# Gate multiplications of the experts move from VectorE to GpSimd, in a fused attention and mixture-of-experts kernel

## The reference

```python
# layer 0: group norm, softmax attention over all 4096 tokens of an image, residual
h = group_norm(x, norm_w, norm_b)              # 32 groups
q, k, v = h @ Wq + bq, h @ Wk + bk, h @ Wv + bv
x = x + (softmax(q @ k.T * C ** -0.5) @ v) @ Wo + bo
# layer 1, on tokens t (b, 4096, 128)
# a: causal attention with one fixed query a head, 8 heads
kv = silu(ln(t) @ W_kv.T);  k, v = kv[..., 0], kv[..., 1]
s = einsum('hd,bthd->bth', q_proj, k)
e = exp(s - cummax(s, axis=1))
t = t + (cumsum(e[..., None] * v) / cumsum(e)[..., None]).mean(heads)
# b: 8 experts, the best two of each token
p = softmax(ln(t) @ router_w + router_b)
top_p, top_i = top_k(p, 2);  top_p /= sum(top_p)
t = t + sum_k top_p[k] * (ln(t) @ expert_w[top_i[k]] + expert_b[top_i[k]])
```

## Time and profile before

| what | value |
|---|---|
| median of 3 runs | 2849.72 us |
| the profiled execution | 2849.48 us, span 2847.4 us |
| mean granted TensorE clock | 0.976 |
| TensorE busy | 2651.4 us, 93% |
| VectorE busy | 2260.2 us, 79% |
| ScalarE busy | 1842.4 us, 65% |
| GpSimd busy | 1766.7 us, 62% |
| moved by DMA | 130.76 MB |

### The profile page before, as it was taken

The page is one execution under the profiler, slowest core; times in us unless marked ns, Lnnn a source line. Parts: engine busy times, 40 slices in busy tenths (PEclk is TensorE's granted clock), DMA queues, the critical chain, the costliest instruction groups (busy, mean ns, idle before and its releaser), DMA issues. The chain is left out here.

```text
span 2847.4 us, 37342 instructions
## 1 busy us (share of the span) xinstructions
PE 2651.4 (93%) x11107; PEld 1909.6 (67%) x11107; DVE 2260.2 (79%) x3453; ACT 1842.4 (65%) x3368; POOL 1766.7 (62%) x1457
## 2 busy tenths in 40 slices
PE   6999999999999999999999999778799899899788
PEld 2888877788877788887788888534355455455443
DVE  5788887788887788887788888427888898898996
ACT  4667676666777666677666666657766666665540
POOL 3677777777776777776777777715544444444430
PEclk8999999999999999999999999989999999999989
DMA  1000000100000100000000000034233323223220
GB/s 63 5 12 8 12 12 8 38 12 12 9 12 8 37 13 10 14 8 8 8 16 8 9 16 8 24 93 164 112 116 109 114 103 135 103 73 131 92 75 26
DMA packets 48378, 130.76 MB, mean 46 GB/s; under 512 B 11472, under 2 KB 14096, under 8 KB 38960
## 3 DMA queue, kind: packets, MB, share of 16 engines
q1 hardware_dynamic: 48176, 128.39, 13.1%
HBM read 110.94 MB, written 17.43 MB: 45 GB/s over the span
## 5 line engine op out<-in xcount | busy, mean ns | idle before, releaser
L184 POOL TENSOR_TENSOR p_lo<-pf,p_hi 128x512 fp32r<-128x512 f32 x1024 | 1319.2, 1291 | 426.3 <-ACT p_hi L409 421.1
L404 ACT ACTIVATE pf<-s_ps 128x512 f32<-128x512 f32 x1024 | 612.8, 598 | 528.6 <-PE s_ps L295 527.7
L499 DVE TENSOR_REDUCE mx<-m_ps 128x1 f32<-128x512 f32 x1024 | 702.7, 688 | 301.8 <-PE m_ps L278 297.6
L515 DVE TENSOR_TENSOR sum_ps<-sum_ps,pf 128x512 f32<-128x512 f32 x960 | 661.9, 690 | 22.7 <-ACT pf L404 22.4
L409 ACT CAST p_hi<-pf 128x512 fp32r<-128x512 f32 x1024 | 627.3, 613 | 0.0
L886 POOL TENSOR_TENSOR acc<-acc,ay 128x512 f32<-128x512 f32 x192 | 255.8, 1332 | 280.8 <-DVE ay L1223 280.4
L293 PE MATMUL s_ps<-q_hi,kd_hi 128*128 128x512 f32 x1024 | 425.4, 415 | 0.0
L278 PE MATMUL m_ps<-kp,q_hi 128*128 128x512 f32 x1024 | 405.4, 398 | 11.1 <-DVE mx L499 5.1
L307 PE MATMUL om_ps<-p_hi,v_hi 128*128 128x512 f32 x1024 | 401.1, 392 | 4.6 <-POOL p_lo L184 4.6
L294 PE MATMUL s_ps<-q_hi,kd_lo 128*128 128x512 f32 x1024 | 399.8, 390 | 0.0
L295 PE MATMUL s_ps<-q_lo,kd_hi 128*128 128x512 f32 x1024 | 399.8, 390 | 0.0
(11 more groups left out here) (206 smaller groups left out, 3605.9 us busy)
## 6 DMA issues: line engine op xcount, KB each, us to landing
bq<-weight_rows SPq DMA_DIRECT2D x64, 1024.0 KB, 4.9
xb<-in_x_dram SPq DMA_DIRECT2D x8, 1024.0 KB, 6.1
rb_sb<-inverse_rows SPq DMA_DIRECT2D x32, 256.0 KB, 3.7
tokens<-xb SPq DMA_DIRECT2D x32, 256.0 KB, 2.0
tp<-tokens SPq DMA_DIRECT2D x32, 256.0 KB, 4.9
rb<-norm_rows SPq DMA_DIRECT2D x32, 256.0 KB, 4.2
tv<-tokens SPq DMA_DIRECT2D x32, 256.0 KB, 5.4
out_dram<-tv SPq DMA_DIRECT2D x32, 256.0 KB, 2.4
```

Of the source, the lines that this page charges most:

```text
L184: nc.gpsimd.tensor_tensor(p_lo[:, r, :], pf[:, r, :], p_hi[:, r, :].bitcast(F32), ALU.subtract).then_inc(lo_done, 1)
L404: nc.scalar.activation(pf[:, g % RING, :], s_ps[:, g % 2, :], ACT.Exp, scale=SCALE).then_inc(exp_done, 1)
L499: nc.vector.tensor_reduce(mx[:, n % 2, sub, chunk:chunk + 1], m_ps[:, j % 2, :], AX.X, ALU.max).then_inc(m_max, 1)
L515: nc.vector.tensor_tensor(sum_ps[:], sum_ps[:], p, ALU.add).then_inc(sum_done, 1)
```

## The change

The gate rows no longer come from TensorE. `hold_gates` also copies the turned gates to `l_sb`, SyncE writes 8 rows of each image to DRAM (`gate_rows`) and brings each block's 8 gates back to all 128 partitions, in two halves of four experts and 1 MB each (`gate_spread`, buffer `gb`, called gate_b in the program). GpSimd multiplies them with the tokens (`gated`), so `spread`, `sel` and `g_ps` go. The two banks of `g_ps` become value banks: `v_ps` has four. On GpSimd the addition of head h - 1 stands in slot h, the last one in slot 0 of the next step. On TensorE expert e stands in slot e + 2 (`X_LAG`), the last two in the next step, and `output` in slot 2. The gates are computed one slot earlier or two, and turned in slot 5. The gate matrix is laid out so that the rows for DRAM are the first eight of a group.

```diff
-    V_LAG, F_LAG = 5, 11
+    V_LAG, F_LAG, X_LAG = 5, 11, 2
...
+        gb = sb("gate_b", [C, 2, HALF, TOK])
...
-        gt = sb("gt", [C, 2, TOK], F32R)
+        gt = sb("gt", [C, TOK], F32R)
...
-        v_ps = psum("v_ps", [C, 2, BANK])
+        v_ps = psum("v_ps", [C, 4, BANK])
...
-        g_ps = psum("g_ps", [C, 2, BANK])
...
+            def gate_rows(s):
+                sp.wait_ge(gr_act, s + 1)
+                for b in range(B):
+                    sp.dma_start(gates_d[s, b, :, :], l_sb[QUAD * b:QUAD * b + E, :]).then_inc(gr_out, 16)
+
+            def gate_spread(i, j):
+                s, b, cols = place(i)
+                sp.wait_ge(gr_out, 16 * B * (s + 1))
+                if i:
+                    sp.wait_ge(xg_pool, (i - 1) * E + HALF * (j + 1))
+                sp.dma_start(gb[:, j, :, :].rearrange("p e n -> p (e n)"),
+                             gates_d[s, b:b + 1, HALF * j:HALF * (j + 1), :].rearrange("o e n -> o (e n)")
+                             .to_broadcast([C, HALF * TOK])).then_inc(gb_in[j], 16)
...
-                if stage(f - 1):
-                    store(f - 1)
...
                 if stage(v + 1):
                     weight_spread(v + 1, 1)
+                if stage(f - 1):
+                    store(f - 1)
+                if stage(f + 1):
+                    if (f + 1) % B == 0:
+                        gate_rows((f + 1) // B)
+                    gate_spread(f + 1, 0)
+                    gate_spread(f + 1, 1)
...
+            def gated(f, e):
+                pool.wait_ge(gb_in[e // HALF], 16 * (f + 1))
+                after(pool, x_pe, f * E + e - 2)
+                if e == 0:
+                    pool.wait_ge(t2_dve, f + 1)
+                nc.gpsimd.tensor_tensor(xg[:, (f * E + e) % 3, :], gb[:, e // HALF, e % HALF, :], tv[:, f % NV, :],
+                                        ALU.mult).then_inc(xg_pool, 1)
...
                 for h in range(HEADS):
+                    if h == 0 and stage(v - 1):
+                        add_head(v - 1, HEADS - 1)
+                    if stage(f):
+                        gated(f, h)
                     if stage(k + 1) and h == 1:
                         scaled(k + 1)
                     if stage(k + 1) and h == 5:
                         low(k + 1)
-                    if stage(v):
-                        add_head(v, h)
+                    if stage(v) and h:
+                        add_head(v, h - 1)
...
-                after(pe, y_dve, v * HEADS + h - 1)
-                project(v_ps[:, h % 2, :], h, 1, v).then_inc(v_pe, 1)
+                after(pe, y_dve, v * HEADS + h - 3)
+                project(v_ps[:, h % 4, :], h, 1, v).then_inc(v_pe, 1)
...
-                    if stage(f) and h == 0:
-                        spread(f, 0)
...
-                    if stage(f) and h + 1 < E:
-                        spread(f, h + 1)
...
-                    if stage(f):
-                        if h == 0:
+                    if stage(f - 1) and h < X_LAG:
+                        expert(f - 1, E + h - X_LAG)
+                    if stage(f) and h >= X_LAG:
+                        if h == X_LAG:
                             expert_bias(f)
-                        expert(f, h)
-                    if norm2_at(j, 2) is not None and h == 7:
+                        expert(f, h - X_LAG)
+                    if norm2_at(j, 2) is not None and h == 5:
                         turn_gates(norm2_at(j, 2))
...
                 act.wait_ge(gt_pe, s + 1)
-                nc.scalar.copy(gt[:, s % 2, :], st_ps[:]).then_inc(gt_act, 1)
+                act.wait_ge(lt_pe, s + 1)
+                nc.scalar.copy(l_sb[:], st_ps[:]).then_inc(gr_act, 1)
+                after(act, x_pe, (B * s - 1) * E + 1)
+                nc.scalar.copy(gt[:], st_ps[:]).then_inc(gt_act, 1)
...
-            def gated(f, e):
-                dve.wait_ge(g_pe, f * E + e + 1)
-                after(dve, x_pe, f * E + e - 2)
-                nc.vector.tensor_tensor(xg[:, e % 3, :], g_ps[:, e % 2, :], tv[:, f % NV, :], ALU.mult).then_inc(xg_dve, 1)
...
-                if stage(f - 1):
-                    output(f - 1)
                 for h in range(HEADS):
+                    if stage(f - 1) and h == X_LAG:
+                        output(f - 1)
                     if stage(v):
                         weigh(v, h)
-                    if stage(f):
-                        if h == 0:
-                            gated(f, 0)
-                        if h + 1 < E:
-                            gated(f, h + 1)
```

More of the change, by code:

```diff
@@ L640, in scan_attention_and_experts @@
     rows_d = nc.dram_tensor("weight_rows", (SUPERS, B * 2, HALF, TOK), F32, kind="Internal").ap()
+    gates_d = nc.dram_tensor("gate_rows", (SUPERS, B, E, TOK), F32, kind="Internal").ap()
     rs_d = nc.dram_tensor("norm_rows", (SUPERS, B, TOK), F32, kind="Internal").ap()
@@ L720, in scan_attention_and_experts @@
             sem(n) for n in ("var2_dve", "msq2_act", "ln2_act", "rst2_act", "gate", "th_act"))
-        gt_pe, gt_act, g_pe, xg_dve, x_pe, out_dve = (
-            sem(n) for n in ("gt_pe", "gt_act", "g_pe", "xg_dve", "x_pe", "out_dve"))
+        gt_pe, gt_act, gr_act, gr_out, xg_pool, x_pe, out_dve = (
+            sem(n) for n in ("gt_pe", "gt_act", "gr_act", "gr_out", "xg_pool", "x_pe", "out_dve"))
+        gb_in = [sem(f"gb_in{i}") for i in range(2)]
+        clr = sem("clr")
         block = ctx.enter_context(nc.Block())
@@ L863, in _ @@
             nc.gpsimd.memset(eb_lo[:].bitcast(F32), 0.0).then_inc(cst2, 1)
+            nc.gpsimd.memset(g32[:], 0.0).then_inc(clr, 1)
             def scaled(i):
@@ L973, in row_sums @@
                     mm.then_inc(s_pe, 1)
[L975 to L981, removed]
             def expert_bias(f):
@@ L985, in expert_bias @@
                 after(pe, out_dve, f)
-                pe.matmul(mo_ps[:], eb_hi[:, b, :], gt[:, s % 2, :], start=True, stop=False)
-                pe.matmul(mo_ps[:], eb_lo[:, b, :], gt[:, s % 2, :], start=False, stop=False)
+                pe.wait_ge(gt_act, s + 1)
+                pe.matmul(mo_ps[:], eb_hi[:, b, :], gt[:], start=True, stop=False)
+                pe.matmul(mo_ps[:], eb_lo[:, b, :], gt[:], start=False, stop=False)
             def expert(f, e):
-                pe.wait_ge(xg_dve, f * E + e + 1)
-                pe.matmul(mo_ps[:], ew[:, e, :], xg[:, e % 3, :], start=False, stop=(e == E - 1)).then_inc(x_pe, 1)
+                pe.wait_ge(xg_pool, f * E + e + 1)
+                pe.matmul(mo_ps[:], ew[:, e, :], xg[:, (f * E + e) % 3, :], start=False, stop=(e == E - 1)).then_inc(x_pe, 1)
             pe.wait_ge(cst1, 5)
@@ L1011, in _ @@
             pe.wait_ge(ec_act, 3)
-            pe.wait_ge(cst3, 6)
-            for j in range(STEPS):
+            pe.wait_ge(cst3, 5)
+            for j in range(STEPS + 1):
                 k, v, f = j, j - V_LAG, j - F_LAG
                 for h in range(HEADS):
-                    if stage(f) and h == 0:
-                        spread(f, 0)
                     if stage(v):
                         value(v, h)
-                    if stage(f) and h + 1 < E:
-                        spread(f, h + 1)
                     if stage(k - 1) and h == 0:
@@ L1075, in silu_value @@
                 act.wait_ge(v_pe, v * HEADS + h + 1)
-                nc.scalar.activation(v_ps[:, h % 2, :], v_ps[:, h % 2, :], ACT.Silu).then_inc(v_act, 1)
+                nc.scalar.activation(v_ps[:, h % 4, :], v_ps[:, h % 4, :], ACT.Silu).then_inc(v_act, 1)
             def old_weight(v, h):
@@ L1091, in hold_logits @@
                 act.wait_ge(lg_pe, s + 1)
+                after(act, gr_out, 16 * B * s)
                 nc.scalar.copy(l_sb[:], st_ps[:]).then_inc(lg_act, 1)
@@ L1166, in _ @@
                         high(k + 1)
-                    if norm2_at(j, 2) is not None and h == 4:
+                    if norm2_at(j, 2) is not None and h == 2:
                         s = norm2_at(j, 2)
@@ L1213, in weigh @@
                 dve.wait_ge(v_act, v * HEADS + h + 1)
-                zv = v_ps[:, h % 2, :]
+                zv = v_ps[:, h % 4, :]
                 nc.vector.tensor_tensor(zv, bq[:, q % 3, h % HALF, :], zv, ALU.mult).then_inc(z_dve, 1)
@@ L1278, in gates @@
                                             ALU.add).then_inc(gate, 1)
-                if slot == 1:
+                if slot == 0:
                     ready(3)
                     first_of(lg, top1, place1, pick1, 3)
-                if slot == 2:
+                if slot == 1:
                     ready(8)
@@ L1287, in gates @@
                     first_of(lg, top2, place2, pick2, 9)
-                if slot == 3:
+                if slot == 2:
                     nc.vector.tensor_tensor(gap[:], top1[:], top2[:], ALU.subtract).then_inc(gate, 1)
@@ L1291, in gates @@
                     nc.vector.tensor_tensor(work, pick1[:], pick2[:], ALU.subtract).then_inc(gate, 1)
-                if slot == 5:
+                if slot == 3:
```

(13 more changed lines are left out.)

14 lines of the change are left out of this document (5 added, 9 removed).

## The result

The changed kernel takes 2835.05 us, median of 6 runs (2833.76 to 2839.51), against 2850.45 for the kernel before: a ratio of 0.9946, 95% interval 0.9933 to 0.9959. It is 15 us faster, clear of noise, where 65 were forecast. It lies 1 us inside the range's upper end of 2836. Its profiled execution took 2835.74 us around a span of 2834.0.

The account below looks back on a forecast made before the run. VectorE and TensorE were nearly full, GpSimd over half empty; after the change waits decide. Full pipeline -51, steps 5 to 10 -11, steps 32 to 36 -12, tail +9: -65 us, to 2785 us, range 2740 to 2836.

Parts of the forecast that it names:

- the full pipeline's -51: Steps 11 to 31, 5.25 cycles of four steps: each cycle falls from 111.2 to 101.5 us, 9.7 less.
- the sum by steps: A full-pipeline cycle: rows step 24.8 us, norm step 29.5, gates step 25.5, plain step 21.7, together 101.5 against 111.2.
- the banks: Four value banks let TensorE run three heads ahead: 0.5 us off norm steps, 0.9 off gates steps, -11 in steps 5 to 10.
- The late gate half: Rows to norm step: gates queue behind weights; GpSimd waits some 8 us, 3 to 3.5 reach TensorE; 3 added per cycle.
- Taken away: VectorE loses 8 `xg` multiplications a step, 98.5 to 83.8 us a cycle; TensorE loses 8 `spread` matmuls, 101.3 to 93.9.
- Added: GpSimd gets 8 multiplications a step at 1.24 us, reaching 91 to 92 us a cycle; new gate transfers add waits.
- Rival C: Contention or start cost holds each GpSimd instruction near 1.67 us, a cycle at 125.4: slower, 2946 us; chance 0.09.
- Rival A: Engines alone decide, banks and slots absorb the waits, a cycle falls to TensorE's 94 us: 2731 us; chance 0.13.
- B: GpSimd sets the pace wherever it was late, with gate waits 105.2 us a cycle: 2817 us; chance 0.21.
- D: No change: what leaves VectorE comes back as waits, needing both B's waits and half of C's contention: 2850 us; chance 0.05.
- The key bank: TensorE waits for ScalarE to clear the one key bank between two keys: 5 to 6 us a cycle, unchanged in kind.
- The other stretches: Outside the full pipeline: -11 us in steps 5 to 10, -12 in steps 32 to 36, +9 in steps 37 to 42.

Follow-up runs that it names:

- e1: Changed kernel with VectorE's `output` moved up from ahead of `weigh` in slot 2 to between `weigh` and `scan` of slot 1: 2810.44 us, 0.9869 to the kernel before.
- e2: Changed kernel with three value banks and two output banks instead of four and one, `output` still in slot 2: 2809.72 us, 0.986 to the kernel before.
- e10: e8 with `output` put back in slot 2 ahead of `weigh`: 2840.63 us, 0.9954 to the kernel before.
- e8: Changed kernel with `output` early, three value and two key banks, tanh one slot later, first gate half ahead of the new weights: 2781.63 us, 0.9759.
- e11: e8 with ScalarE's tanh back at slot 2 as in the changed kernel: 2785.64 us, 0.9763 to the kernel before.
- e5: e1 with three value banks and two key banks in place of four and one: 2807.0 us, 0.9846 to the kernel before.
- e4: Changed kernel with the first gate half issued ahead of `weight_rows` in a rows step: 2833.43 us, 0.9943 to the kernel before.
- e9: Changed kernel, its own banks, with `output` early, tanh one slot later and first gate half ahead of the new weights: 2786.72 us, 0.9764 to the kernel before.
- e6: e1 with two value banks instead of four: 2815.84 us, 0.9881 to the kernel before.

## Why the prediction was wrong

**The step that failed is the full pipeline's -51 in the sum by steps.** It took what each engine sheds (3.7 us a step on VectorE, 1.9 on TensorE) off each step's length and added the waits for the gates. It had the banks let TensorE run up to three heads ahead and the experts' two slots absorb the late gates. It left out, and so put at nothing, what the same edit ties: `expert_bias` and `output` both in slot 2, with one bank between them, on engines of which one runs several us behind the other. That wait is 8.4 us a cycle, with slow clock after it. So a cycle lost 1.5 to 1.8 us instead of 9.7, and the -51 came out as some -9.

**What stood in its place, sized.** Late `output` against early: 22 us in the changed kernel (e1, and e2 by another way), 56 with the other waits out of the way (e10 against e8). The late gate half: 24 us once `output` is early (e11 against e5), of it 3.2 us a cycle in the full pipeline where 3 were forecast, so that this price was right; in the changed kernel itself nothing (e4). These prices overlap and can't be added.

**What stays open.** The output wait explains 22 of the 50 us between 2785 and 2835. e1 still has a cycle of 105.3 us, against 101.5 forecast. What holds it there isn't the key bank alone (e5), nor the tanh as far as e8 beside e11 can tell. Without the late gate half the forecast would have been some 16 us lower, 2769 (an estimate, 3 us in each of 5.25 cycles), while e8, e9 and e11 take 2782 to 2787. That they lie where the forecast of 2785 lay is luck.

**Taken away.** Right in size: VectorE 84.7, TensorE 95.6 us a cycle. That a head saves less than the instruction's 0.60 us fits these 84.7 us. Wrong in the banks: waits of `weigh` for ScalarE went up, not down, and even with `output` early four banks against two are 5 us in steps 5 to 10 and 0.4 a cycle (e6).

**Added.** Right: `xg` at a mean of 1.296 us, GpSimd at 88.5. Rival C, contention, is excluded by that row. GpSimd's wait of 8.8 us once a cycle was forecast at 8; that 2 to 4 of it reach an expert was wrong in the changed kernel (0.52) and right in e1 (2.93). Rival A, engines alone, falls by these waits. The measured time lies between rivals B (2817) and D (2850), and neither mechanism is the cause. GpSimd doesn't set the pace (B): it waits 7.3 us a cycle for TensorE, and e4 takes its gate wait away for nothing. D is right that what leaves VectorE comes back as waits, but it needed B's waits and half of C's contention.

**The key bank.** The forecast had "an estimate of 5 to 6 us a cycle, unchanged in kind", and did not add it to the sum. The size is right, 5.1 and 10 in e1; "unchanged" is not, since TensorE waited 0.4 us there before. Giving the keys a second bank bought nothing (e5).

**The other stretches** were right in kind: -6.4 for -11 in steps 5 to 10, -10.6 for -12 in steps 32 to 36, +6.2 for +9 in the tail.

That 2835 lies inside the range is luck too: the range had no case for this wait, and its upper end is 1 us away.

## What to carry to other kernels

When a producer is moved back by some slots, list for each buffer that it writes who must free it, and in which slot of which engine that stands, and count how far this engine runs behind: the same slot number on two engines is not the same time. Before adding banks to one tile, look for the bank that is filled once a step and read out by an instruction queued behind others. And test repairs together as well as alone: the gate half was worth nothing alone and 24 us once the wait for `output` was gone.

## What was not expected of the hardware

A wait of 4.9 us on TensorE cost more than itself: the granted clock was 0.50 in the four microseconds around its end and 0.66 in the next four, and the pair of an expert's matmuls took 1.91 us instead of 1.02. A shorter wait can do the same and need not. Behind 2.10 us of wait for the bias at 2422.14 the clock was 0.50 from 2424 to 2426 and the pair took 1.72 us; behind 2.11 us at 2314.02 it stayed at 1.00. Of the 109.7 us of the cycle the mean clock was 0.94, against 0.98 before.
